# Head weights prepared by ScalarE and GpSimd, factors on GpSimd, joined value tiles, seven banks in the ramp, one ternary step on ScalarE

## What is computed

```python
x = x + tanh(g_xattn[0]) * xattn(layernorm(x), ctx)
x = x + tanh(g_ffn[0])   * ffn(layernorm(x))
# xattn: q, qx, k, v = e4m3(ln(x)/in_scale)*in_scale @ W.T * w_scale      (16, 16, 8, 8 heads of 128)
#        kx, vx = ctx @ w_kv_x.T;  q, k, qx, kx = layernorm per head of 128 columns
#        core = softmax(q k / sqrt(128)) v;  xout = softmax(qx kx / sqrt(128)) vx
#        out  = e4m3(concat(core, xout)/smooth) @ wproj.T * scales
# ffn:   down(silu(a) * b), both products with ternary weights and int8-like activations:
#        w -> clip(round(w / mean|w|), -1, 1) * mean|w|
```

## Time and profile before

| | us |
|---|---|
| median of 3 runs (range) | 2000.99 (1998.81 to 2005.33) |
| the profiled execution, its own time | 2004.23 |
| its span, first to last instruction | 2002.4 |
| start to the first row maximum | 138.3 |
| head groups 0 to 5 (slots 0 to 95) | 355.7 |
| head groups 6 to 18 | 572.8 |
| head groups 19 to 22 | 207.0 |
| head groups 23 to 26 | 177.6 |
| head groups 27 to 31 | 191.0 |
| rest | 360.2 |

### The profile page before, as it was taken

The page is one execution under the profiler, slowest core; times in us unless marked ns, Lnnn a source line. Parts: engine busy times, 40 slices in busy tenths (PEclk is TensorE's granted clock), DMA queues, the critical chain, the costliest instruction groups (busy, mean ns, idle before and its releaser), DMA issues.

```text
span 2002.4 us, 35210 instructions
## 1 busy us (share of the span) xinstructions
PE 1668.2 (83%) x11147; PEld 1013.2 (51%) x11164; DVE 1746.9 (87%) x4062; ACT 1188.1 (59%) x2963; POOL 1017.8 (51%) x1327
## 2 busy tenths in 40 slices
PE   1467777768899998989999777999999958999996
PEld 0344444445566665556666444555566623444442
DVE  5769989999999989999999999999999955777774
ACT  2025556546788886778797656677777851222222
POOL 3476666666766665676665455555666521000000
PEclk7678999898999999999999999999999978999997
DMA  2236666767999998889999878899998797333200
GB/s 86 84 119 148 145 150 133 171 151 175 197 225 195 211 227 185 179 191 226 202 204 197 183 173 180 191 212 214 209 188 163 135 237 242 88 92 88 74 17 16
DMA packets 664285, 325.48 MB, mean 163 GB/s; under 512 B 551328, under 2 KB 594464, under 8 KB 663072
## 3 DMA queue, kind: packets, MB, share of 16 engines
q1 hardware_dynamic: 664096, 323.17, 71.6%
HBM read 140.61 MB, written 48.23 MB: 94 GB/s over the span
## 4 chain that ended last, share of the span: by engine, by line
DVE 50%; PE 27%; POOL 9%; issue 7%; DMA 3%; ACT 3%; SPq 0%; POOLq 0%; DVEq 0%; ACTq 0%
DVE pp L948 9%; DVE nmx L938 9%; PE psum L687 5%; PE psum L662 5%; PE psum L645 4%; PE psum L633 3%; PE psum L605 3%; PE psum L704 3%; DVE xh L921 3%; DVE wbt L826 2%; DMA pt<-pp 2%; PE psum L612 2%; POOL raw L1353 2%; DVE cc L962 2%; DVE ast L907 2%
## 5 line engine op out<-in xcount | busy, mean ns | idle before, releaser
L633 PE MATMUL psum<-qk 128*128 128x512 f16 x1536 | 427.7, 388 | 74.5 <-DVE pp L948 71.1
L605 PE MATMUL psum<-wbt,xqt 128*128 128x256 f16 (+1 forms) x4096 | 413.8, 251 | 53.6 <-DVE xh L921 39.7
L1236 ACT ACTIVATE psum<-psum,nmx 128x512 f32<-128x512 f32 x512 | 341.1, 666 | 143.6 <-DVE nmx L938 139.3
L605 PEld LDWEIGHTS psum<-wbt,xqt 128*128 128x128 f16 x4096 | 334.5, 100 | 167.3 <-DVE xh L921 45.2
L948 DVE SCALAR_TENSOR_TENSOR pp<-psum,prs,pp 128x512 f16<-128x512 f32 x512 | 377.8, 738 | 16.5 <-ACT pp L1247 16.5
L1247 ACT ACTIVATE pp<-psum,prs 128x512 f16<-128x512 f32 x512 | 351.2, 686 | 20.9 <-DMA pt<-pp 20.9
L938 DVE TENSOR_REDUCE nmx<-psum 128x1 f32<-128x512 f32 x512 | 342.8, 670 | 17.9 <-PE psum L633 17.2
L1242 ACT ACTIVATE prs<-psm 128x1 f32<-128x1 f32 x512 | 108.1, 211 | 258.7 <-DVE psm L943 257.3
L1429 POOL TENSOR_TENSOR qk<-y,qk 128x512 f16<-128x512 f32 x192 | 233.7, 1217 | 16.0
L633 PEld LDWEIGHTS psum<-qk 128*128 128x128 f16 x1536 | 142.8, 99 | 166.2 <-DVE pp L948 79.8
L645 PE MATMUL psum<-pt,vx 128*128 128x512 f16 x768 | 203.3, 389 | 24.5 <-ACT cy L1255 21.5
(11 more groups left out here) (169 smaller groups left out, 2801.6 us busy)
## 6 DMA issues: line engine op xcount, KB each, us to landing
wbt<-ws SPq DMA_DIRECT2D x192, 256.0 KB, 3.6
ws<-wbt SPq DMA_DIRECT2D x64, 256.0 KB, 3.9
catd<-cy SPq DMA_DIRECT2D x64, 256.0 KB, 3.3
raw<-in_wgu SPq DMA_DIRECT2D x64, 256.0 KB, 3.6
wbt<-catd SPq DMA_DIRECT2D x8, 2048.0 KB, 9.8
raw<-in_w SPq DMA_DIRECT2D x32, 384.0 KB, 3.8
pt<-pp SPq DMA_TRANSPOSE x512, 3.5
raw<-in_wp SPq DMA_DIRECT2D x32, 256.0 KB, 3.7
```

The source lines that it names most:

```text
L605: ins = e.matmul(bank[:, o0:o0 + c1 - c0], xv[:, v, kt * 512 + tt * 128:kt * 512 + (tt + 1) * 128], wb[i][:, h, kt, c0:c1], start=kt == 0 ...
L633: ins = e.matmul(SB(n), qk[i][:, jq, u, ss], qk[i][:, jk, w, :], start=k == 0, stop=k == 2)
L1236: e.activation(SB(n), SB(n), ACT.Exp, bias=nmx[:, k], accum_out=psm[:, k]).then_inc(s["exp"], 1)
```

## The change

For each of the four 128x768 pieces of a group: DVE only sums and makes -mean times ratio (two operations); ACT centres and scales each head's 128 columns in place with one activation that has a bias and a scale per partition (`w_mid`, five with bias and scale, one with scale alone, spread over two slots), then writes the upper half in one activation of 768 columns (`w_hi`); GpSimd subtracts it to get the lower half (`w_lo`, one operation of 768 columns). For kv alike: four activations of 128 columns and one of 512 in place, one of 1024, and two subtractions of 512 columns on GpSimd (`kv_lo`). The steps of a piece stand one slot apart, and `w_dn` is now raised by GpSimd. `PREP_LOAD` puts each load one slot ahead of its sum.

`group_factors` has four operations and stands on GpSimd. `vs` and `vx` become one tile `vv`, so `v_hi` and `v_lo` are one operation of 256 columns each instead of two of 128. In the ramp, up to slot -5, the ring takes the four score banks too, and `stats` come ahead of `norms` in DVE's order. The first of the three operations of a ternary job (times scale, plus 12582912) goes from DVE to ACT. Ahead of the loop the pieces of group 0 are interleaved with the turning of x, the context's factor comes ahead of that of kv, and one raw load is issued ahead of the eight stores.

```diff
-VSCALE = 2.0 ** -11
-XSCALE = 2.0 ** -14
+VSCALE = 2.0 ** -14
...
-PREP_HI = (-10, -6, -4, -1)
-KV_AT = {"part": 2, "spread": 3, "whole": 4, "fac": 5, "hi": 5, "lo": 6}
+PREP_LOAD = (-13, -10, -7, -4, -1)
+PREP = {"mean": 1, "near": 2, "far": 3, "hi": 4, "lo": 5}
+KV_AT = {"part": 0, "spread": 0, "whole": 1, "fac": 2, "mid": 3, "hi": 4, "lo": 5, "lo2": 6}
+RAMP = -4
...
+    bank, older = {}, {}
+    last = {k: ("X0", 0) for k in range(4)}
+    turn = [5, 6, 7, 0, 1, 2, 3]
+    for n, use in order:
+        if n >= RAMP:
+            turn = [k for k in turn if k >= 5]
+        k = turn.pop(0)
+        turn.append(k)
+        bank[use] = k
+        if k in last:
+            older[use] = last[k]
+        last[k] = use
...
-                for it, kt in prep_at(n - 3):
-                    if kt < 3:
-                        load_raw(it, kt + 2)
-                    elif it + 1 < NG:
-                        load_raw(it + 1, 0)
+                for it, kt in loads_at(n):
+                    if (it, kt) != (1, 0):
+                        load_raw(it, kt)
...
+                    for it in kv_at(n - 3 - k, "lo"):
...
+                if n < 4:
+                    read(*RAMP_LAST[n])
...
-            def group_factors(it):
-                b, g = divmod(it, NG)
-                f = kfac[it % 4]
-                q.wait_ge("cxf", b + 1)
-                q.wait_ge("wxf", g + 1)
-                q.wait_ge("b_rs", (it - 3) * 4)
-                q.wait_ge("o_y", (it - 3) * 4)
-                q.done(e.tensor_scalar(f[:, 0:1], cmx[:, b, 1:2], wmx[:, g, 1:2], 2.0 ** -20, ALU.mult, ALU.mult))
-                q.done(e.reciprocal(f[:, 1:2], f[:, 0:1]))
-                q.done(e.tensor_scalar(f[:, 1:2], f[:, 1:2], (EPS * D) ** 0.5, None, ALU.mult))
-                e.tensor_tensor(eps6[it % 4][:, 5:6], f[:, 1:2], f[:, 1:2], ALU.mult)
-                e.tensor_scalar(f[:, 2:4], aco[:, 16 + 2 * g:18 + 2 * g], f[:, 0:1], 8.0,
-                                ALU.mult, ALU.mult).then_inc(s["gf"], 1)
...
-                q.done(e.tensor_reduce(wmean[:, k % 2, 0:h], src, AX, ALU.add))
-                e.tensor_scalar(wmean[:, k % 2, 0:h], wmean[:, k % 2, 0:h], 1.0 / D, None, ALU.mult).then_inc(s["wm"], 1)
-            def prep_w(it, kt):
-                k, i = it * 5 + kt, it % 2
-                r = raw[k % 2]
-                for c0, c1, v in COLS:
-                    q.wait_ge("w_hi", (it * 4 + kt) * 4 + v + 1)
-                    ins = e.scalar_tensor_tensor(wb[i][:, 1, kt, c0:c1], r[:, c0:c1], ratio[:, v, kt:kt + 1],
-                                                 wb[i][:, 0, kt, c0:c1], ALU.mult, ALU.subtract)
-                ins.then_inc(s["w_dn"], 1)
+                return e.tensor_reduce(wmean[:, k % 2, 0:h], src, AX, ALU.add)
+            def head_means(it, kt):
+                k = it * 5 + kt
+                q.done(head_sums(it, kt))
+                e.scalar_tensor_tensor(wmean[:, k % 2, :], wmean[:, k % 2, :], -1.0 / D, ratio[:, kt, 0:5],
+                                       ALU.mult, ALU.mult).then_inc(s["wm"], 1)
...
-                e.scalar_tensor_tensor(vs[ix][:, tt, 1, :], bank[:, 128:256], VSCALE, vs[ix][:, tt, 0, :],
-                                       ALU.mult, ALU.subtract)
-                e.scalar_tensor_tensor(vx[ix][:, tt, 1, :], bank[:, 384:512], XSCALE, vx[ix][:, tt, 0, :],
-                                       ALU.mult, ALU.subtract).then_inc(s["vx_lo"], 1)
+                e.scalar_tensor_tensor(vv[ix][:, tt, 1], bank.rearrange("p (a b) -> p a b", a=2)[:, :, 128:256], VSCALE,
+                                       vv[ix][:, tt, 0], ALU.mult, ALU.subtract).then_inc(s["vx_lo"], 1)
...
-                    q.done(e.tensor_scalar(f, f, wsc[:, k:k + 1], MAGIC, ALU.mult, ALU.add))
...
+                for tiles, at in ((stats, n - 1), (norms, n - 2)) if n < RAMP else ((norms, n - 2), (stats, n - 1)):
+                    tiles(at)
...
+            def w_mid(it, kt, first, last):
+                k = it * 5 + kt
+                q.wait_ge("wm", k + 1)
+                for h in range(first, last):
+                    cols = raw[k % 2][:, h * 128:(h + 1) * 128]
+                    if h < 5:
+                        ins = e.activation(cols, cols, ACT.Identity, bias=wmean[:, k % 2, h:h + 1], scale=ratio[:, kt, h:h + 1])
+                    else:
+                        ins = e.activation(cols, cols, ACT.Copy, scale=ratio[:, kt, h:h + 1])
+                if last == 6:
+                    ins.then_inc(s["wc"], 1)
+            def w_hi(it, kt):
+                k, i = it * 5 + kt, it % 2
+                q.wait_ge("wc", k + 1)
+                q.wait_ge("gb", (it - 1) * 4)
+                q.wait_ge(f"w_st{i}", 128 * (it // 2))
+                e.activation(wb[i][:, 0, kt, :], raw[k % 2][:, 0:768], ACT.Copy).then_inc(s["w_hi"], 1)
+            def kv_mid(it):
+                k = it * 5 + 4
+                q.wait_ge("wm", k + 1)
+                r = raw[k % 2][:].rearrange("p (k n) -> p k n", k=4)
+                for kt in range(4):
+                    e.activation(r[:, kt, 0:128], r[:, kt, 0:128], ACT.Identity, bias=wmean[:, k % 2, kt:kt + 1],
+                                 scale=wfa[:, it:it + 1])
+                e.activation(r[:, :, 128:256], r[:, :, 128:256], ACT.Copy, scale=wfa[:, it:it + 1]).then_inc(s["wc"], 1)
+            def kv_hi(it):
+                k, i = it * 5 + 4, it % 2
+                q.wait_ge("wc", k + 1)
+                q.wait_ge("gb", (it - 1) * 4)
+                q.wait_ge(f"w_st{i}", 128 * (it // 2))
+                e.activation(wkvb[i][:, 0], raw[k % 2][:].rearrange("p (k n) -> p k n", k=4), ACT.Copy).then_inc(s["w_hi"], 1)
...
-                e.activation(vs[ix][:, tt, 0, :], bank[:, 128:256], ACT.Copy, scale=VSCALE)
-                e.activation(vx[ix][:, tt, 0, :], bank[:, 384:512], ACT.Copy, scale=XSCALE).then_inc(s["vh"], 1)
+                e.activation(vv[ix][:, tt, 0], bank.rearrange("p (a b) -> p a b", a=2)[:, :, 128:256], ACT.Copy,
+                             scale=VSCALE).then_inc(s["vh"], 1)
...
+                elif what == "tern":
+                    k = 6 if src == "wgu" else 7
+                    q.wait_ge(f"raw_ld{i}", JV[f"raw_ld{i}", K0 + m])
+                    q.wait_ge("l_sc", 1)
+                    e.activation(f, f, ACT.Identity, bias=magic[:], scale=wsc[:, k:k + 1]).then_inc(s["l_t1"], 1)
...
-            def center(it, kt):
-                k = it * 5 + kt
-                r, h = raw[k % 2], 4 if kt == 4 else 5
-                cols = r[:].rearrange("p (k n) -> p k n", k=4)[:, :, 0:128] if kt == 4 else \
-                    r[:, 0:640].rearrange("p (k n) -> p k n", k=5)
-                q.wait_ge("wm", k + 1)
-                e.tensor_tensor(cols, cols, wmean[:, k % 2, 0:h].unsqueeze(2).broadcast_to([128, h, 128]),
-                                ALU.subtract).then_inc(s["wc"], 1)
-                q.wait_ge("wc", k + 1)
...
+            def group_factors(it):
+                b, g = divmod(it, NG)
+                f = kfac[it % 4]
+                q.wait_ge("cxf", b + 1)
+                q.wait_ge("wxf", g + 1)
+                q.wait_ge("o_y", (it - 3) * 4)
+                e.tensor_scalar(f[:, 0:1], cmx[:, b, 1:2], wmx[:, g, 1:2], 2.0 ** -20, ALU.mult, ALU.mult)
+                q.done(e.tensor_scalar(f[:, 1:2], cfa[:, b:b + 1], wfa[:, g:g + 1], 1.0, ALU.mult, ALU.mult))
+                e.tensor_scalar(eps6[it % 4][:, 5:6], f[:, 1:2], f[:, 1:2], EPS * D, ALU.mult, ALU.mult)
+                e.tensor_scalar(f[:, 2:4], aco[:, 16 + 2 * g:18 + 2 * g], f[:, 0:1], 8.0,
+                                ALU.mult, ALU.mult).then_inc(s["gf"], 1)
...
-            def prep_w(it, kt):
+            def w_lo(it, kt):
                 k, i = it * 5 + kt, it % 2
-                r = raw[k % 2]
-                q.wait_ge(f"raw_ld{k % 2}", JV[f"raw_ld{k % 2}", k])
-                q.wait_ge("gb", (it - 1) * 4)
-                q.wait_ge(f"w_st{i}", 128 * (it // 2))
-                q.wait_ge("const_ready", 1)
-                center(it, kt)
-                for c0, c1, v in COLS:
-                    e.tensor_scalar(wb[i][:, 0, kt, c0:c1], r[:, c0:c1], ratio[:, v, kt:kt + 1], 1.0,
-                                    ALU.mult, ALU.mult).then_inc(s["w_hi"], 1)
-            def kv_hi(it):
-                k, i = it * 5 + 4, it % 2
-                q.wait_ge("wxf", it + 1)
-                q.wait_ge("gb", (it - 1) * 4)
-                q.wait_ge(f"w_st{i}", 128 * (it // 2))
-                center(it, 4)
-                e.tensor_scalar(wkvb[i][:, 0], raw[k % 2][:].rearrange("p (k n) -> p k n", k=4), wfa[:, it:it + 1], 1.0,
-                                ALU.mult, ALU.mult).then_inc(s["wx_hi"], 1)
+                q.wait_ge("w_hi", k + 1)
+                e.tensor_tensor(wb[i][:, 1, kt, :], raw[k % 2][:, 0:768], wb[i][:, 0, kt, :],
+                                ALU.subtract).then_inc(s["w_dn"], 1)
+            def kv_lo(it, half_):
```

(6 more changed lines are left out.)

228 lines of the change are left out of this document (126 added, 102 removed).

## The result

The changed kernel takes **1943.8 us** (median of four runs, 1941.0 to 1946.5) beside 2002.3 of the kernel before in the same comparison: ratio 0.9708, 95% interval 0.9686 to 0.9731. It is faster by 58.5 us, where 104 were forecast, and 1943.8 lies just beyond the upper end of the range, 1940. The profiled execution has a span of 1940.9 us, 61.5 less than before.

The account below looks back on a forecast made before the run. VectorE, busy 87% of the span, was taken as the bound, with ScalarE next in head groups 0 to 5. Gains of 15 + 42 + 47 = 104 us off 2004.2 gave 1900, or 1897 for the median; range 1860 to 1940.

Parts of the forecast that it names:

- I charge nothing and keep 10 in the upper end: Head groups 0 to 5: VectorE waits of 6 to 18 us for late loads, covered by its 48 us of idle time.
- its gains of 6, 21 and 26 us: Smallest gains forecast for the start, head groups 0 to 5 and the later groups; together they give 1948 us.
- a round of 9.7 us per buffer: Start: a piece passes VectorE, ScalarE twice, GpSimd and SP; with two buffers 4.9 us per piece, 34 for seven.
- Who is next: Head groups 0 to 5: ScalarE at 282 us, above VectorE's 265 and TensorE's 235; 90% full gives 313, gain 42.
- the coupling that the prediction named: Head groups 0 to 5: longer GpSimd subtractions could hold VectorE operations by an exclusive lock; the sum stayed unchanged.
- The surcharge for a source in SBUF: Head groups 0 to 5: extra latency on 183 ScalarE activations, 0.07 us each, 13 us, counted only in the bound.
- I take these as equal: Start: seven banks and 1.9 us less VectorE work per piece balance the longer round of pieces; gain 15 us.
- Later groups: Behind head group 5: gains of 16 (groups 6 to 18), 15 (19 to 22), 15 (23 to 26) and 1; sum 47.
- (b): Rival, head groups 0 to 5: ScalarE's queue stops the softmax, the stage keeps its 356 us; 1939 us, chance 0.19.
- (c): Rival, slower: VectorE's sums wait a whole landing, 3.9 us, at each of 35 pieces; 2034 us, chance 0.04.
- (a): Rival, head groups 0 to 5: ScalarE's work is covered, 291 us, ramp's banks pay 10 more; 1864 us, chance 0.18.
- (d): Rival, whole kernel: the change does not do what it says, VectorE's time becomes equal waits; 2001 us, chance 0.01.

Follow-up runs that it names:

- three kernels: The changed kernel with four raw buffers (1893.1 us), with three and loads three slots earlier (1893.7), and with four and kv's spread matmul one slot later (1890.5).
- the twelve: The twelve kernels that do the changed kernel's work in head groups 19 to 22; that stage takes 189.8 to 193.2 us in them, the middle 191.4.
- the last experiment: Changed kernel with four raw buffers, early loads and a piece's centring halves in one slot, upper and lower half one slot earlier: 1914.6 us, ratio 0.9562.
- four buffers and the later matmul: Changed kernel with four raw buffers, loads six slots earlier, and kv's spread matmul one slot later: 1890.5 us, ratio 0.9425.

## Why the prediction was wrong, point by point

**The step that failed** is in the part on GpSimd and SP of head groups 0 to 5: "For four pieces of five there is a full slot between subtraction and load", and "I charge nothing and keep 10 in the upper end". The piece's path was named there with every link of it, `w_dn` behind the rsqrt, SP's load behind `w_dn`, 3.9 us of landing. What it said of the second piece, whose load stands in the slot of kv's subtraction, came true: VectorE waits 1.5 to 3.0 us there, five times, 11.3 us. What went wrong is, first, that for the other pieces a slot of distance in the program was read as a slot of time; they wait another 22.3 us. The engines don't stand at the same slot: in the chain above GpSimd's part of a slot begins when VectorE's statistics of that slot are done, 2 us in, and its power and subtraction take 2.9 us more, while SP already waits at the next slot's load. SP waited 43.3 us at 16 of 26 loads, VectorE 33.6 us at 20 of 26 pieces. Second, the 48 us of idle time on VectorE were to cover the wait. They did not: the wait came on top, and VectorE is idle 74 of 352 us. The price by the runs is 35.9 us in head groups 0 to 5, not nothing. Nor are the 10 us in the upper end: its gains of 6, 21 and 26 us give 1948, and with the 10 it would be 1958. The same working had a round of 9.7 us per buffer, 4.9 per piece, for the ramp. That adds the durations alone. In the schedule each step stands in a slot of its own, and the round measured is 20.0 us, the whole of the six slots in which a buffer comes up again: there is no slack left. The Trainium skill, "DMA: Bandwidth & Descriptors", section "Anatomy of one DMA — SWDGE (gpsimd) path", says that a DMA's wait on a semaphore is done by the issuing sequencer before dispatch; SP's rows above agree, with up to 6.1 us at one load and the transposes behind it.

**Who is next.** The forecast put head groups 0 to 5 at 313 us with ScalarE next. With the landings out of the way the stage takes 316.3, 314.8 and 311.2 us in three kernels, so the sum behind the missed wait was right in size. That was luck in part, since its reason was wrong: leaving out 34 us of ScalarE work moves the stage 4 us. VectorE at 277 of 316 us (88%, as group 3 in the earlier trace rows) is the nearer bound. ScalarE was forecast at 282 and came to 272, VectorE at 265 and came to 277: two errors that cancel.

**Prices.** ScalarE's activations: forecast 0.48, 0.38 and 0.79 us, measured medians 0.492, 0.404 and 0.853. GpSimd's subtraction: forecast 1.8, measured 1.64. ScalarE's total: 282 forecast, 272.0 measured. VectorE: 265 forecast, 277.8 measured. Of these 12.8 us, 7.8 are the step that makes -mean times ratio (L829, and L844 for kv), which was taken as unchanged and takes 12.5 us instead of 4.7. L829 takes 0.17 us in eleven of its twenty times here and 0.53 to 1.09 in nine; each of the nine began beside a GpSimd operation of 512 columns with two inputs and ended 0.01 to 0.03 us behind its end:

```profile
276.69 1.16 POOL L1480 TENSOR_TENSOR qk<-y,qk 128x512 f16<-128x512 f32 x1
```

```profile
277.32 0.55 DVE L829 SCALAR_TENSOR_TENSOR wmean<-wmean,ratio 128x5 f32<-128x5 f32 x1
```

This is the coupling that the prediction named and set at nothing because GpSimd's total falls; what counts is what stands beside the small operation, not the total.

The surcharge for a source in SBUF, which the Trainium skill ("VectorE: DVE Perf Modes", the section on the TRN2 errata) gives and which I priced at 0.043 us by it and 0.07 us by a row, is 0.01 to 0.02 us on the small activations and 0.06 on the wide one against the prices made from the PSUM rows, so the trace doesn't show one fixed amount. The one pair of the same form, 512 columns with two per-partition operands, has 0.789 from PSUM and 0.817 in place in `raw` (the ternary step, L1299), 0.028 apart. The row of 653 ns behind the 0.07 also sums its input (`accum_out`), which the reading left out.

**Start.** 15 forecast, 18.8 measured, first row maximum at 119.5 and not 123. But "I take these as equal" hid two wrong terms: the seven banks bring 1.6 us, not an amount that balances the round, and the round cost 15 (slot 0 at 104.65 with four buffers), 9 by the buffers alone (110.4) and 6 by the earlier loads, two of them ahead of the eight stores.

**Later groups.** 47 forecast, 39.9 measured, within its bounds. Groups 6 to 18: VectorE lost 22 us of work (26 forecast), the time only 7.4, and TensorE was busy 531 of the 573 us before and 526 of 565 after; the bound of 5 was nearer than the 16 taken. Groups 19 to 22 gave 17.2, or 15.6 beside the middle of the twelve, for 15. The sum is right there, its terms are not: 9 us of VectorE for the ternary step came to 12.1, and undoing the step costs 15.7 to 17.3 us there (11.8 when it is made alone). In return 16 us were set for the factors in groups 19 to 26, and undoing the factors costs 5.8 to 7.4 us. Groups 23 to 26: 40.65 us each forecast, 41.3 measured.

**The rivals.** (b) gives 1939, near the measured 1944, and its sign, ScalarE below 85% in head groups 0 to 5 with VectorE idle too, was there (77% and 79%). Its mechanism was not: the centring left out gains nothing. With the landings gone, a dense order of ScalarE's does cost (the last experiment), but that is not what held this kernel. The mechanism was that of (c), GpSimd's late `w_dn` and a landing at the sum, at 1.7 us for each of 20 waits in head groups 0 to 5 instead of 3.9 for each of 35 pieces. (c) was taken as all or nothing, so the middle, which happened, had no case and no chance of its own. (a) and (d) didn't occur. With the missed 51 us the forecast's 1897 would be 1948; without the wait the kernel runs in 1893. That both fit within 5 us is partly the luck of errors that cancel, as above.

Not tried: the joined values undone alone. Their term is 1.5 us, below what a comparison of this kernel can tell.

## What to carry to other kernels

When work moves from one engine to a chain of several, write down the round of each buffer, with every queue that it passes and what stands ahead of it there, and compare it with the slots it has, for each piece and not for the worst one. A slot of distance in the program is none in time when the two engines don't run at the same point of it; the remedy is a third buffer and an earlier load (50 us here by the medians), for which memory that is filled only later can serve. And after the change look first whether any engine is full: if none is, the waits name a chain, and taking work off an engine outside that chain gives nothing.

## What was not expected of the hardware

A part of what a wait elsewhere costs, or seems to cost, is TensorE's granted clock. The matmuls of head groups 0 to 5 (1794 in the trace) took 271.3 us at a mean granted clock of 0.91 (a mean over its two levels, 1.2 and 2.4 GHz) in the changed kernel, 261.0 at 0.93 with four buffers and the later matmul, and 258.9 at 0.95 with four buffers; so 12 of the 35.9 us between the first and the last are TensorE's own time. The clock does not follow TensorE's idle time in step: it is idle 80.9, 50.2 and 57.4 us of these three stages, and the kernel before, idle for 88.1 us, has 0.93. And in head groups 19 to 22 the same work with the same idle time (24.6 to 25.1 us) had 0.97 to 0.99 from one kernel to the next, and 3 us of difference by it. What moves it isn't settled by these runs; a difference of that size between two kernels says nothing without their clocks.

A small VectorE operation can be held by a GpSimd operation that runs beside it. The two of the same form in the changed kernel, 0.17 and 0.55 us, differ by what GpSimd had under way.

A wait in SP's queue alone cost nothing: 32 us of them stand in the kernel with four buffers that runs 51 us faster.
